# Layer 1's last sums: which queue loads the partial sums and stores the final rows

## The chip, the cores and the metric

The kernel runs on one core of one Trainium2 chip. The metric is device time of one execution in microseconds (us). The engines are called by their short names: PE is TensorE (PEld its weight loads), DVE is VectorE, ACT is ScalarE, POOL is GpSimd, SP is SyncE. SP computes nothing here: it waits for semaphores and issues transfers. A transfer can be issued by SP, by ACT or by POOL; each engine handles its own instructions strictly in order, so a wait in front of one instruction holds everything behind it.

## The reference

The input is 4 batches of 2048 tokens with 256 values each. Two half-weight mixture-of-experts layers stand around one attention layer:

```
x = x + 0.5 * ffn(layernorm(x))      # layer 0
x = x + attention(layernorm(x))
x = x + 0.5 * ffn(layernorm(x))      # layer 1, gives the result
# ffn: two of 16 experts for each token, mixed by softmax of the two router scores, plus a shared expert
# attention: the first 256 tokens attend causally to themselves, the other 1792 to 64 compressed tokens
```

So each row of the result is (row before layer 1) + 0.5 x (shared expert) + two expert results with their weights.

## The kernel before

A batch is handled as 8 *pairs* (`PB`), a pair being 2 x 128 rows of 256 values, 256 KB. The work runs in 16 phases in the order of a plan, with a fence between them. A phase T (tokens) normalises a batch's rows, routes them and computes the shared expert; it stores x + shared part in the DRAM tensor `partial_sums` (`acc_v`). A phase E (experts) takes the normalised rows by slot, in pairs of slot pages, through their experts, and stores `slot_results`. A phase A (attention) first adds the two expert results of layer 0 to each row of a batch and then runs attention on it. The phase C at the end does the last sums of batch 3.

The last sums of the other batches, layer 1's rows, are hidden in other phases. For pair n of such a batch they are: load the partial sums into `last_x[n % 2]` (a part of `normalised_rows`), gather four blocks of 128 expert results into `last_gath[n % 2]` (for even n a part of `normalised_rows`, for odd n `gathered_last_results`), four instructions of DVE (`last_sum`, at L1273 and L1278, which count `last_out`), and store the finished pair to `out`. Two places do them:

- the attention phase of batch 3, here called **A3**, does the 16 pairs of batches 0 and 1. DVE adds pairs 2i-2 and 2i-1 at the end of step i of its loop (i = 1 to 7) and pairs 14 and 15 after the loop. POOL also gathers layer 0's results for the attention's own rows there (`gathered_results`), two pairs ahead of their use;
- the second expert phase of layer 1, here called **E14**, does the 8 pairs of batch 2. DVE's loop body of four expert pairs ends with two sums in its last four turns. POOL gathers the rows of the expert pairs there too (L722), four ahead of PE, and puts a last pair behind every second one of them from pair 36 of 48 on.

In the kernel before, POOL does every transfer of the last sums. `last_pair(ph, n)` waits until pair n-2 is summed, stores it (L667), waits until that store has landed (`sums_stored`, since pair n is loaded over it), loads the partial sums of pair n (L680) and issues the four gathers of pair n (L655). SP has in A3 only the loads and stores of the attention's own rows, and in E14 nothing.

Of the kernel before, what the change touches and what calls it, by code (L numbers as in the profile page):

```python
# [35 lines left out]
PB = TB // 2  # L36
# [28 lines left out]
NS = 4  # L65
# [56 lines left out]
def macaron_kernel(nc, x_in, wq, wk, wv, wo, w1, b1, w2, b2, rw_t, rbias, up, gate, down,  # L122
                   shg_t, shu_t, shd_t, out, plan):
    ctx = ExitStack()
    with ctx:
# [254 lines left out]
        phases = []  # L380
# [81 lines left out]
        def _(sp):  # L462
# [19 lines left out]
            def store_rows(ph, i, s):  # L482
                sp.wait_ge(a_out.sem, a_out.done(ph["a"] + i))
                sp.dma_start(acc_v[ph["b"] * PB + i], outs[:, s]).then_inc(outs_stored[s].sem, 16)

            def load_tokens(ph, pairs):
# [43 lines left out]
            for ph in phases:  # L530
# [19 lines left out]
                if ph["kind"] == "T":  # L550
                    tokens(ph)
                elif ph["kind"] == "A":
                    for i in range(NS, PB):
                        load_rows(ph, i, i % NS)
                    for i in range(5, PB + 5):
                        if i == PB + 4:


                            sp.wait_ge(c_out.sem, c_out.done(ph["c"] + PB - 1))
                            for s in range(NS):  # L560
                                sp.wait_ge(outs_stored[s].sem, used(ph, s, s))
                            load_tokens(phases[ph["n"] + 1], range(NS))
# [13 lines left out]
        def _(gp):  # L576
# [82 lines left out]

            def last_pair(ph, n):  # L660

                lasts = ph["last"]
# [8 lines left out]
                if n < PB * len(lasts):  # L671
                    last, l = lasts[n // PB], lasts[0]["l"] + n
                    if n % PB == 0:
                        results_stored(1, last["b"])
                    if n == 0:
                        gp.wait_ge(phase_done["pe"].sem, ph["n"])
                        for s in range(NS):
                            gp.wait_ge(norm_stored[s].sem, 32 * ph["tokens_before"])
                    gp.wait_ge(sums_stored[n % 2].sem, 8 * (l - n % 2))
                    gp.dma_start(last_x[:, n % 2], acc_v[last["b"] * PB + n % PB]).then_inc(sums_in[n % 2].sem, 16)  # L680
                    gather_pair(last_gath[n % 2], last_in[n % 2], 1, last["b"], n % PB)

            def gather(ph):

# [6 lines left out]
                        for n in range(2 * i - 8, 2 * i - 6):  # L691
                            last_pair(ph, n)
                if ph["last"]:
                    for n in range(PB, PB * len(ph["last"]) + 2):
                        last_pair(ph, n)

            def gather_all(ph):
# [11 lines left out]
            def slot_rows(ph):  # L709
# [16 lines left out]
                            last_pair(ph, (i - begin) // 2)  # L726
                    first += part["pairs"]
                if ph["last"]:
                    for n in range((ph["pairs"] - begin) // 2, PB + 2):
                        last_pair(ph, n)  # L730

            def build(ph, n):
# [1181 lines left out]
```

## Time and profile before

| | |
|---|---|
| three runs, median (lowest to highest) | 2016.77 us (2015.26 to 2021.91) |
| the profiled execution, its own time | 2013.89 us |
| its span in the trace | 2012.2 us |
| PE busy | 1480.4 us (74%) |
| DVE busy | 1047.0 us (52%) |
| POOL busy | 876.3 us (44%) |
| chain that ended last | PE 53%; DVE 14%; POOL 13%; issue 10%; DMA 4% |
| stores to `out` by POOL (DMA out<-normalised_rows) in that chain | 3.0% |

Busy times overlap; no engine is busy through the whole span, so the time is made of stretches with different limits. The chain is the sequence of work in which each piece was released by the one before it; what stands in it sets the time. POOL's rows for a transfer give how long POOL took to issue it, not how long the data travelled.

### The profile page before, as it was taken

The page shows a single profiled execution, that of the slowest core. Times are in us where ns is not written, and L with a number is a line of the kernel's source. Part 1 is how long each engine was busy: PE and PEld are TensorE (multiplying, and loading weights), DVE is VectorE, ACT ScalarE, POOL GpSimd, SP SyncE. Part 2 cuts the span into 40 slices and gives each one's busy share as a digit, 9 for nine tenths or more (in the row PEclk, how much of TensorE's full clock was granted, in tenths as well). Part 3 has the DMA queues.
Part 4 walks back from the last instruction along what each step waited for, and adds up shares of the span by engine and source line. Part 5 has one row for each costly group of instructions (what it writes and reads, how often), then busy time and mean ns, then how long its engine had stood idle before and what let it go on. Part 6 is the DMA issues. An engine that isn't in the chain of part 4 may idle for free.

```text
span 2012.2 us, 35562 instructions
## 1 busy us (share of the span) xinstructions
PE 1480.4 (74%) x11274; PEld 1247.8 (62%) x11275; DVE 1047.0 (52%) x3253; ACT 617.5 (31%) x1254; POOL 876.3 (44%) x1108
## 2 busy tenths in 40 slices
PE   4797787999967779578767779698674447799650
PEld 3787677988854548455654559587543327698540
DVE  4657546544434755556734766243553547474332
ACT  2333223444423323233212323244321103244220
POOL 4563486655532200210272006655135463756656
PEclk9897798999976889688877889799786767799775
DMA  4732224556541122210231021356223352256555
GB/s 116 225 104 65 84 79 126 167 164 157 161 136 43 48 74 74 81 39 24 90 121 43 27 74 63 107 160 156 84 64 110 105 157 77 87 156 176 147 146 170
DMA packets 166002, 215.71 MB, mean 107 GB/s; under 512 B 18800, under 2 KB 143856, under 8 KB 165872
## 3 DMA queue, kind: packets, MB, share of 16 engines
q0 software_dynamic: 32256, 90.22, 17.0%
q1 hardware_dynamic: 87920, 79.74, 12.3%
q10 hardware_dynamic: 45696, 44.05, 6.6%
q8 instruction: 78, 1.28, 0.3%
q14 instruction: 52, 0.43, 0.1%
HBM read 119.56 MB, written 94.37 MB: 106 GB/s over the span
## 4 chain that ended last, share of the span: by engine, by line
PE 53%; DVE 14%; POOL 13%; issue 10%; DMA 4%; ACT 4%; another core or an unknown queue 2%; ACTq 0%; DVEq 0%; POOLq 0%; SPq 0%
PE bank L1444 8%; PE bank L1455 7%; PE bank L1594 7%; PE bank L1457 6%; PE bank L1456 6%; PE bank L1515 4%; DMA out<-normalised_rows 3%; POOL queries_high L739 2%; POOL normalised_rows L655 2%; POOL gathered_last_results L655 2%; DVE bn_stats L1042 2%; POOL rows_and_results L722 2%; PE bank L1846 2%; DVE score_maxima L1328 2%
## 5 line engine op out<-in xcount | busy, mean ns | idle before, releaser
L722 POOL DMA_INDIRECT rows_and_results<-normalised_by_token,rows_of_slots x336 | 319.7, 952 | 215.4 <-PE bank L1444 131.5
L655 POOL DMA_INDIRECT gathered_results<-slot_results,slot x128 | 122.0, 953 | 389.4 <-DVE combined_rows L1278 282.8
L1226 DVE TENSOR_TENSOR rows_transposed_low<-bank,rows_transposed_high 128x512 fp32r<-128x512 f32 x168 | 116.0, 691 | 270.2 <-ACT rows_transposed_high L812 178.6
L1455 PE MATMUL bank<-expert_gate_up_high,rows_transposed_high 128*128 x672 | 210.3, 313 | 47.1 <-DVE rows_transposed_low L1226 27.1
L737 POOL TENSOR_SCALAR keys_high<-iota,place_in_page_of_choice 128x128 fp32r<-128x128 f32 x96 | 57.6, 600 | 330.1 <-DVE place_in_page_of_choice L1165 322.7
L1456 PE MATMUL bank<-expert_gate_up_low,rows_transposed_high 128*128 x672 | 194.3, 289 | 0.0
L1457 PE MATMUL bank<-expert_gate_up_high,rows_transposed_low 128*128 x672 | 194.1, 289 | 0.0
L1594 PE MATMUL bank<-expert_down,hidden_work 128*128 x672 | 186.6, 403 | 0.5
L1455 PEld LDWEIGHTS bank<-expert_gate_up_high,rows_transposed_high 128*128 128x128 f32 x672 | 132.8, 198 | 60.0 <-issue 58.5
L1455 PE MATMUL bank<-rows_transposed_high,shared_gate_up_high 128*128 128x256 f32 x512 | 159.1, 311 | 0.3 <-DVE hidden_work L1001 0.3
L1444 PE MATMUL bank<-identity,hidden_work 128*128 128x128 f32 x464 | 96.8, 308 | 78.0 <-ACT hidden_work L766 29.8
L1456 PE MATMUL bank<-rows_transposed_low,shared_gate_up_high 128*128 128x256 f32 x512 | 152.8, 298 | 0.0
L1457 PE MATMUL bank<-rows_transposed_high,shared_gate_up_low 128*128 128x256 f32 x512 | 152.6, 298 | 0.0
L812 ACT ACTIVATE rows_transposed_high<-bank 128x512 fp32r<-128x512 f32 x168 | 100.4, 598 | 154.6 <-ACT rows_and_results L827 65.5
L827 ACT ACTIVATE rows_and_results<-bank 128x512 f32<-128x512 f32 x168 | 100.5, 598 | 153.8 <-PE bank L1594 129.8
L1456 PEld LDWEIGHTS bank<-expert_gate_up_low,rows_transposed_high 128*128 128x128 f32 x672 | 133.3, 198 | 0.0
L1594 PEld LDWEIGHTS bank<-expert_down,hidden_work 128*128 128x128 f32 x672 | 120.8, 200 | 19.1 <-issue 8.2
L1457 PEld LDWEIGHTS bank<-expert_gate_up_high,rows_transposed_low 128*128 128x128 f32 x672 | 132.7, 197 | 0.0
L1444 PE MATMUL bank<-identity,rows_and_results 128*128 128x128 f32 x672 | 109.0, 288 | 23.2 <-DMA rows_and_results<-normalised_by_token,rows_of_slots 23.2
L1515 PE MATMUL bank<-shared_down,hidden_work 128*128 128x256 f32 x512 | 121.3, 380 | 0.0
L766 ACT ACTIVATE normalised_rows<-rows_and_results,minus_mean_by_deviation,rstd 128x256 f32<-128x256 f32 x128 | 68.7, 591 | 155.5 <-DVE minus_mean_by_deviation L1081 146.7
L739 POOL TENSOR_SCALAR queries_high<-iota,page_of_choice,token_of_batch_plus_one 128x48 fp32r<-128x48 f32 (+2 forms) x192 | 115.9, 604 | 0.0
(277 smaller groups left out, 3754.9 us busy)
## 6 DMA issues: line engine op xcount, KB each, us to landing
slot_results<-rows_and_results ACTq DMA_DIRECT2D x168, 256.0 KB
partial_sums<-rows_and_results SPq DMA_DIRECT2D x96, 256.0 KB, 2.1
rows_and_results<-partial_sums SPq DMA_DIRECT2D x72, 256.0 KB, 4.3
normalised_by_token<-normalised_rows SPq DMA_DIRECT2D x64, 256.0 KB, 2.5
rows_and_results<-in_L_attn_hidden_states SPq DMA_DIRECT2D x32, 256.0 KB, 3.3
normalised_rows<-partial_sums POOLq DMA_DIRECT2D x24, 256.0 KB
out<-normalised_rows POOLq DMA_DIRECT2D x24, 256.0 KB, 2.7
rows_and_results<-normalised_by_token,rows_of_slots POOLq DMA_INDIRECT x336
```

The lines of the kernel that those rows point to most:

```text
L655: gp.indirect_dma_start(into[:, t, k, :], None, ys[part], bass.IndirectOffsetOnAxis(ap=slot[:, b, k, 2 * i + t:2 * i + t + 1], axis=0))\
L722: gp.indirect_dma_start(rows[:, i % NS, t, :], None, norm_d, bass.IndirectOffsetOnAxis(ap=listed[:, page:page + 1], axis=0))\
L739: gp.tensor_scalar(page_one[n % BUILT][:, 0:width], iota_f[:, 0:width], pagef[:, k, t:t + 1], token_f[:, t:t + 1], ALU.is_equal, ALU.mult) ...
L812: act.activation(flat(xt_h[:, k]), bank[k][:], ACT.Copy)\
L827: act.activation(flat(outs[:, s]), bank[6 + s % 2][:], ACT.Copy)\
L1226: dve.tensor_tensor(flat(xt_l[:, k]), bank[k][:], flat(xt_h[:, k]).bitcast(F32), ALU.subtract)\
L1444: return pe.transpose(out_, in_, ident[:])
L1455: pe.matmul(out_, lh, rh, start=first, stop=False)
L1456: pe.matmul(out_, lh, rl, start=False, stop=False)
L1457: return pe.matmul(out_, ll, rh, start=False, stop=last)
L1515: m = pe.matmul(bank[6 + s % 2][:, t * D:(t + 1) * D], work[:, 1 + i % 2, h, t * P:(t + 1) * P], sd[:, h, :], start=h == 0, stop=h == SH / ...
L1594: m = pe.matmul(bank[6 + k][:, t * D:(t + 1) * D], ht[:, k, t * P:(t + 1) * P], ed[:, ds(e, 1), :].rearrange("p a d -> p (a d)"), start=Tr ...
```

## The change

The loads of the partial sums and the stores of the finished rows go from POOL to SP. POOL keeps the gathers; in front of the gathers of pair n it now waits only until pair n-2 is summed. SP gets `load_sum` and `store_sum`. In A3 it puts two of each between two stores of the attention's rows; in E14 it runs them through in a loop of its own. The loads of pairs 0 and 1 are issued at once. What is computed, the buffers and DVE's order are as before.

```diff
+            def load_sum(ph, n):
+                last, l = ph["last"][n // PB], ph["last"][0]["l"] + n
+                if n == 0:
+                    for s in range(NS):
+                        sp.wait_ge(norm_stored[s].sem, 32 * ph["tokens_before"])
+                sp.wait_ge(sums_stored[n % 2].sem, 8 * (l - n % 2))
+                sp.dma_start(last_x[:, n % 2], acc_v[last["b"] * PB + n % PB]).then_inc(sums_in[n % 2].sem, 16)
+
+            def store_sum(ph, n):
+                last, l = ph["last"][n // PB], ph["last"][0]["l"] + n
+                sp.wait_ge(last_out.sem, last_out.done(l))
+                sp.dma_start(out_v[last["b"] * PB + n % PB], last_x[:, n % 2]).then_inc(sums_stored[n % 2].sem, 16)
...
                 elif ph["kind"] == "A":
...
-                    for i in range(5, PB + 5):
-                        if i == PB + 4:
...
-                        store_rows(ph, i - 5, (i - 5) % NS)
+                    if ph["last"]:
+                        load_sum(ph, 0)
+                        load_sum(ph, 1)
+                    for i in range(PB - 1):
+                        if i:
+                            store_rows(ph, i - 1, (i - 1) % NS)
+                        if ph["last"]:
+                            for n in (2 * i, 2 * i + 1):
+                                store_sum(ph, n)
+                                load_sum(ph, n + 2)
+                    store_rows(ph, PB - 2, (PB - 2) % NS)
+                    next_tokens(ph)
+                    store_rows(ph, PB - 1, (PB - 1) % NS)
+                    if ph["last"]:
+                        for n in (2 * PB - 2, 2 * PB - 1):
+                            store_sum(ph, n)
+                elif ph["kind"] == "E" and ph["last"]:
+                    load_sum(ph, 0)
+                    load_sum(ph, 1)
+                    for n in range(PB):
+                        store_sum(ph, n)
+                        if n + 2 < PB:
+                            load_sum(ph, n + 2)
...
             def last_pair(ph, n):
...
-                def store(n):
-                    last, l = lasts[n // PB], lasts[0]["l"] + n
-                    gp.wait_ge(last_out.sem, last_out.done(l))
-                    gp.dma_start(out_v[last["b"] * PB + n % PB], last_x[:, n % 2]).then_inc(sums_stored[n % 2].sem, 16)
...
                 if n >= 2:
-                    store(n - 2)
...
-                    gp.wait_ge(sums_stored[n % 2].sem, 8 * (l - n % 2))
-                    gp.dma_start(last_x[:, n % 2], acc_v[last["b"] * PB + n % PB]).then_inc(sums_in[n % 2].sem, 16)
-                    gather_pair(last_gath[n % 2], last_in[n % 2], 1, last["b"], n % PB)
+                    gp.wait_ge(last_out.sem, last_out.done(l - 2))
+                gather_pair(last_gath[n % 2], last_in[n % 2], 1, last["b"], n % PB)
```

`next_tokens` holds the waits and loads that stood under `if i == PB + 4`, unchanged.

POOL's instructions in A3 before the change, from the gathers of last pair 1 to the load for last pair 4 (L667 is the store, L680 the load of partial sums, `gathered_results` the attention's own gathers):

```order
L655 DMA gathered_last_results<-slot_results0,slot 128x256 x4
L655 DMA gathered_results<-slot_results1,slot 128x256 x4
L667 DMA out<-normalised_rows 128x2x256
L680 DMA normalised_rows<-partial_sums 128x2x256
L655 DMA normalised_rows<-slot_results0,slot 128x256 x4
L667 DMA out<-normalised_rows 128x2x256
L680 DMA normalised_rows<-partial_sums 128x2x256
L655 DMA gathered_last_results<-slot_results0,slot 128x256 x4
L655 DMA gathered_results<-slot_results1,slot 128x256 x4
L667 DMA out<-normalised_rows 128x2x256
L680 DMA normalised_rows<-partial_sums 128x2x256
```

The same place of POOL after the change, where all gathers are L689:

```order
L689 DMA gathered_last_results<-slot_results0,slot 128x256 x4
L689 DMA gathered_results<-slot_results1,slot 128x256 x4
L689 DMA normalised_rows<-slot_results0,slot 128x256 x4
L689 DMA gathered_last_results<-slot_results0,slot 128x256 x4
L689 DMA gathered_results<-slot_results1,slot 128x256 x4
```

The stores and loads are gone from between the gathers, and 12 gathers in a row stand where two stores and two loads parted them.

SP's instructions in A3 before the change, where L480 loads the attention's rows, L484 stores them and L489 loads the next phase's rows:

```order
L480 DMA rows_and_results<-partial_sums 128x2x256 x8
L484 DMA partial_sums<-rows_and_results 128x2x256 x7
L489 DMA rows_and_results<-partial_sums 128x2x256 x4
L484 DMA partial_sums<-rows_and_results 128x2x256
L489 DMA rows_and_results<-partial_sums 128x2x256 x4
```

SP's first instructions in A3 after the change, with L492 the load and L497 the store of a last sum:

```order
L480 DMA rows_and_results<-partial_sums 128x2x256 x8
L492 DMA normalised_rows<-partial_sums 128x2x256 x2
L497 DMA out<-normalised_rows 128x2x256
L492 DMA normalised_rows<-partial_sums 128x2x256
L497 DMA out<-normalised_rows 128x2x256
L492 DMA normalised_rows<-partial_sums 128x2x256
L484 DMA partial_sums<-rows_and_results 128x2x256
L497 DMA out<-normalised_rows 128x2x256
L492 DMA normalised_rows<-partial_sums 128x2x256
```

Each L484 from the first on now has two stores and two loads of last sums ahead of it, and the stores of pairs 14 and 15 stand between the last L484 and the last loads of the next phase's rows.

## Rows read from the trace of the kernel before

**Rows 1.** Chain of waits in A3: start us, us, what.

```profile
1508.37 2.92 DMA out<-normalised_rows
...
1530.41 2.69 DMA gathered_results<-slot_results,slot
...
1537.53 2.57 DMA out<-normalised_rows
...
1559.25 2.73 DMA gathered_results<-slot_results,slot
...
1569.35 2.58 DMA out<-normalised_rows
```

**Rows 2.** Who waited for whom, 1430 to 1665 us: total us, times, longest.

```profile
POOL normalised_rows L680 <- DMA out<-normalised_rows: 33.7, 14, 4.1
```

**Rows 3.** Busy us of PE, PEld, DVE, ACT, POOL; then clock, DMA share, GB/s.

```profile
1508.00:1662.00 154.00, 67.65 (x596) 45.76 (x596) 71.83 (x155) 22.09 (x45) 84.31 (x93) 0.69 0.40 124
1853.00:1958.00 105.00, 62.78 (x356) 54.36 (x355) 35.45 (x83) 24.18 (x48) 64.48 (x70) 0.77 0.55 152
```

**Rows 4.** Timeline of POOL in A3: start us, us, instruction, idle before it.

```profile
1556.74 0.95 POOL L655 DMA_INDIRECT gathered_results<-slot_results,slot  x1 [0.30 <-issue]
...
1587.20 0.76 POOL L667 DMA_DIRECT2D out<-normalised_rows  x1
...
1605.25 0.76 POOL L667 DMA_DIRECT2D out<-normalised_rows  x1
```

**Rows 5.** Timeline of DVE in two attention phases, batch 2's (1146 to 1195) and A3.

```profile
1146.64 2.48 DVE L1328 TENSOR_REDUCE score_maxima<-bank 128x8 f32<-128x512 f32 x4
...
1154.36 0.69 DVE L1313 TENSOR_TENSOR rows_transposed_low<-bank,rows_transposed_high 128x512 fp32r<-128x512 f32 x1 [1.56 <-ACT rows_transposed_high L864]
...
1176.67 2.48 DVE L1328 TENSOR_REDUCE score_maxima<-bank 128x8 f32<-128x512 f32 x4 [3.72 <-PE bank L1816]
...
1194.98 0.69 DVE L1355 TENSOR_TENSOR rows_and_results<-bank,combined_rows 128x512 f32<-128x512 f32 x1 [3.34 <-PE bank L1673]
...
1570.56 2.48 DVE L1328 TENSOR_REDUCE score_maxima<-bank 128x8 f32<-128x512 f32 x4
...
1581.44 0.69 DVE L1313 TENSOR_TENSOR rows_transposed_low<-bank,rows_transposed_high 128x512 fp32r<-128x512 f32 x1 [4.73 <-ACT rows_transposed_high L864]
```

**Rows 6.** Timeline of DVE at A3's end and the next phase's start.

```profile
1663.14 0.87 DVE L1278 SCALAR_TENSOR_TENSOR normalised_rows<-gathered_last_results,weights,normalised_rows 128x256 f32<-128x256 f32 x2
...
1668.41 0.16 DVE L1081 SCALAR_TENSOR_TENSOR minus_mean_by_deviation<-mean,rstd 128x4 f32<-128x4 f32 x1
```

**Rows 7.** Who waited for whom, 1800 to 2012 us (E14's end and C).

```profile
POOL normalised_rows L680 <- DMA out<-normalised_rows: 17.1, 6, 4.0
```

**Rows 8.** Timeline of POOL in E14, around the first last pair, and the last gather.

```profile
1850.61 0.95 POOL L722 DMA_INDIRECT rows_and_results<-normalised_by_token,rows_of_slots  x1 [0.94 <-PE bank L1444]
...
1949.98 0.95 POOL L655 DMA_INDIRECT gathered_last_results<-slot_results,slot  x1 [0.30 <-issue]
```

**Rows 9.** Timeline of DVE in E14, the sums of pairs 1, 5, 6 and 7.

```profile
1875.32 0.87 DVE L1278 SCALAR_TENSOR_TENSOR normalised_rows<-gathered_last_results,weights,normalised_rows 128x256 f32<-128x256 f32 x2
...
1932.51 0.88 DVE L1278 SCALAR_TENSOR_TENSOR normalised_rows<-gathered_last_results,weights,normalised_rows 128x256 f32<-128x256 f32 x2
...
1945.90 0.87 DVE L1273 SCALAR_TENSOR_TENSOR normalised_rows<-normalised_rows,weights 128x256 f32<-128x256 f32 x2
...
1954.00 0.88 DVE L1278 SCALAR_TENSOR_TENSOR normalised_rows<-gathered_last_results,weights,normalised_rows 128x256 f32<-128x256 f32 x2
```

**Rows 10.** Timeline of SP in A3: one store of attention rows.

```profile
1652.06 0.36 SPq L484 DMA_DIRECT2D partial_sums<-rows_and_results  x1
```

**Rows 11.** Us from issue to landing: SP's loads, POOL's stores, SP's four loads together.

```profile
rows_and_results<-partial_sums SPq DMA_DIRECT2D x72, 256.0 KB, 4.3
...
DMA to landing us min/median/max: 2.6/2.7/4.6
...
DMA to landing us min/median/max: 5.3/5.3/5.3
```

More of the change, by code:

```diff
@@ L484, in store_rows, with next_tokens @@
                 sp.dma_start(acc_v[ph["b"] * PB + i], outs[:, s]).then_inc(outs_stored[s].sem, 16)
+            def load_sum(ph, n):
[9 more added lines that the diff above has]
+                sp.dma_start(out_v[last["b"] * PB + n % PB], last_x[:, n % 2]).then_inc(sums_stored[n % 2].sem, 16)
+            def next_tokens(ph):
+                sp.wait_ge(c_out.sem, c_out.done(ph["c"] + PB - 1))
+                for s in range(NS):
+                    sp.wait_ge(outs_stored[s].sem, used(ph, s, s))
+                load_tokens(phases[ph["n"] + 1], range(NS))
             def load_tokens(ph, pairs):
@@ L554, in _ @@
                         load_rows(ph, i, i % NS)
-                    for i in range(5, PB + 5):
-                        if i == PB + 4:
[L559 to L562, printed above, removed]
-                        store_rows(ph, i - 5, (i - 5) % NS)
+                    if ph["last"]:
[21 more added lines that the diff above has]
+                            load_sum(ph, n + 2)
                 elif ph["kind"] == "C":
@@ L660, in last_pair @@
             def last_pair(ph, n):
-                lasts = ph["last"]
-                def store(n):
-                    last, l = lasts[n // PB], lasts[0]["l"] + n
-                    gp.wait_ge(last_out.sem, last_out.done(l))
-                    gp.dma_start(out_v[last["b"] * PB + n % PB], last_x[:, n % 2]).then_inc(sums_stored[n % 2].sem, 16)
-                if n >= 2:
-                    store(n - 2)
[L671 to L678, printed above, removed]
-                    gp.wait_ge(sums_stored[n % 2].sem, 8 * (l - n % 2))
-                    gp.dma_start(last_x[:, n % 2], acc_v[last["b"] * PB + n % PB]).then_inc(sums_in[n % 2].sem, 16)
-                    gather_pair(last_gath[n % 2], last_in[n % 2], 1, last["b"], n % PB)
+                last, l = ph["last"][n // PB], ph["last"][0]["l"] + n
+                if n % PB == 0:
+                    results_stored(1, last["b"])
+                if n == 0:
+                    gp.wait_ge(phase_done["pe"].sem, ph["n"])
+                    for s in range(NS):
+                        gp.wait_ge(norm_stored[s].sem, 32 * ph["tokens_before"])
+                if n >= 2:
+                    gp.wait_ge(last_out.sem, last_out.done(l - 2))
+                gather_pair(last_gath[n % 2], last_in[n % 2], 1, last["b"], n % PB)
             def gather(ph):
@@ L693, in gather @@
                 if ph["last"]:
-                    for n in range(PB, PB * len(ph["last"]) + 2):
+                    for n in range(PB, PB * len(ph["last"])):
                         last_pair(ph, n)
@@ L728, in slot_rows @@
                 if ph["last"]:
-                    for n in range((ph["pairs"] - begin) // 2, PB + 2):
+                    for n in range((ph["pairs"] - begin) // 2, PB):
                         last_pair(ph, n)
```

## The prediction

> **What bounds the kernel now.** I read the whole chain of waits first. It is mixed, but it has two long stretches in which PE hardly occurs and POOL's gathers alternate with stores to `out`: A3 from 1508 us to its end at 1664, and E14 from 1853 to 1955. The busy time by stretch [rows 3] shows why they are worth a look: POOL is the busiest engine in both (84.3 of 154 us, 64.5 of 105), PE is idle for much of them, and its granted clock is a mean of 0.69 and 0.77, between its two levels of 1.2 and 2.4 GHz. No engine is full, so a loop of waits sets the pace.
>
> The chain of A3 [rows 1] shows the loop. DVE finishes pair 0 and POOL stores it at 1508.37. The twelfth gather behind that store, the last one for the attention's own pair 6, is issued at 1530.41. DVE takes it 2.7 us later, adds pair 6, then the last sums 2 and 3, and the next store goes out at 1537.53. The waits [rows 2] price POOL's part: 14 times it stood until a store had landed before it could load over it, 33.7 us. In E14 POOL waits the same way 6 times, 17.1 us [rows 7].
>
> **What POOL loses, per last pair.** One gather takes 0.95 + 0.30 = 1.25 us of POOL [rows 4], four are 5.0 us. A store and a load cost the rest: two stores of neighbouring pairs stand 18.05 us apart for two pairs [rows 4], 9.0 per pair, so 4.0 us per pair go to store, landing and load. Those 4 us leave POOL for all pairs that have a store ahead of them.
>
> **A3, cycle by cycle.** Nothing changes before 1508.37, since pair 0's sum is released by attention work. Then:
>
> - *Step 1 to 2.* Twelve gathers in a row: the last is issued 11 x 1.25 = 13.8 us behind the release, 14.0 with a slower first one, where it now takes 1530.41 - 1508.37 = 22.0. That saves 8.0. *Step 2 to 3*: 1559.25 - 1537.53 = 21.7 against 14.0, 7.7 more. What is late next, DVE's own step, is 11.6 us from its maxima to its split of the transposed rows (1570.56 to 1581.44 + 0.69 [rows 5]) and about 1.2 before that, 12.8, still under 14.0 + 2.7. So the gathers still set the pace, and the store at 1569.35 [rows 1] becomes a release at about 1553.6.
> - *Step 4.* POOL now has only last pairs, 8 gathers or 10 us a step. Pair 7's last gather is issued at 1553.6 + 8.8 and lands by 1565.1. DVE starts its maxima at 1570.56 - 15.7 = 1554.9; from there to the end of the split is 8.4 us in the attention phase of batch 2, which has no last sums (1146.64 to 1154.36 + 0.69), and 11.6 in A3, where PE had cooled down [rows 5]. A last sum is two instruction pairs of 0.8 us, 1.6. I take the nearer condition, a PE that waits less: 1554.9 + 8.4 + 3.2 = 1566.5. DVE has become the bound.
> - *Step 5* the same, 11.6 more, 1578.1. *Step 6* has no split; pair 11's gathers end 0.3 + 8.8 + 2.7 = 11.8 us behind the release by sum 8 (1576.5), so 1588.3, and sum 11 is done at 1589.9. *Step 7 and the end*: from step 7's maxima to the last attention sum batch 2 needs 1194.98 + 0.69 - 1176.67 = 19.0 us [rows 5]; sums 12 and 13 fit into DVE's idle time in it (pair 13 has landed by about 1598), 14 and 15 come behind: 1589.9 + 19.0 + 3.2 = 1612.1.
>
> The phase now ends at 1663.14 + 0.87 = 1664.0 [rows 6]. That saves 51.9 us. With 11.6 instead of 8.4 in two steps it is 45.5; with landings of 4.6 instead of 2.7 us [rows 11] in the four places where gathers still bind, another 7.6 goes. I take 50.
>
> **E14.** Until the first last pair POOL keeps up: an expert pair takes it two gathers and a wait for PE, 0.94 + 0.95 + 0.30 + 0.95 = 3.14 us [rows 8]. From 1850.61 + 2.5 = 1853.1 on, 54 gathers are left (32 of last pairs, 22 of expert pairs). In a row the last would be issued at 1853.1 + 53 x 1.25 = 1919.4, against 1949.98. That 30.6 us is the most there is. Two other limits take some back. The sum of pair 1 (done at 1876.2 [rows 9]) was not late by its gathers, so POOL may slip some 2.5 us against expert pairs that aren't transposed yet. And after the sum of pair 5 DVE has four expert pairs to do before pair 6's: 1945.90 - 1933.4 = 12.5 us [rows 9]. Pair 5's last gather is the 44th: 1853.1 + 53.8 + 2.7 = 1909.6, sum done at 1911.2 to 1913.7; then 12.5 and 3.2: sum 7 is done at 1926.9 to 1929.4, against 1954.00 + 0.88 = 1954.9. That saves 25.5 to 28, I take 27. PE's floor (12 pairs x 3.14 + 8 sums x 1.6 = 50.6 us) is far below these 75. What follows, results stored and then C, has its own gathers and keeps its length.
>
> **What is added to SP.** It gets 24 loads and 24 stores, each some 0.4 us of its queue (0.36 in [rows 10]), which is nearly idle here. The cost lies in the order. In A3 each store of attention rows (L484) now stands behind two waits for landed stores. DVE waits for such a store only four pairs later, so it has a step's worth of cover and more. At the end, the store of pair 6's rows waits for the store of sum 13 to land: about 1599.7 + 0.4 + 2.7 + 0.4 = 1603.2, against some 1602 when the row is ready; the loads of the next phase's first rows go out behind it and land by 1611, 5.3 us at the slowest [rows 11]. They are needed at 1612. I cost it at 0; without that cover it is 1 to 3 us. The last store lands about 2.7 us after the phase, and ACT, which waits for it, needs the norms only 4.4 us after it (1664.0 to 1668.4 [rows 6]): 0.
>
> The load of pair n still waits until pair n-2 has been stored over the same buffer, now on SP. With a landing time of X, two pairs in a row are 3X + 3.8 us (a store, a load, a store, a load, three landings in series, 2.2 us of issue and release, the sum's 1.6). At 2.7 us, POOL's median for such stores [rows 11], this is 11.9, beside gathers that need 11.8 + 1.6: hidden, and I cost it at 0. SP's own loads take 4.3, but most are issued in bunches.
>
> **The rule that speaks against it.** The rows say that a store lands 2.7 us after POOL's issue, and as late as 4.6 behind gathers in E14 and A3 [rows 11], which could come from standing in POOL's queue. The Trainium skill (DMA: Bandwidth & Descriptors, "Queues, rings and completion order") says that a transfer's semaphore increment lands only after every earlier write of the same DMA engine, across its queues. By that, a store on SP would be held up by gathers as much as one on POOL. The trace cannot tell, as no store to `out` has left SP beside gathers. What it would do here is the second rival.
>
> **Sum.** 50 + 27 = 77 us from the profiled execution's 2013.9 gives 1936.9. The median of the runs is 2.9 us above that execution; I forecast between the two bases, 1938.
>
> **Rivals.**
>
> - *DVE's steps stay slow in A3*, because PE still waits for the sums and its clock stays low. Steps 4 to 6 then take 11.6 + 3.2 = 14.8: step 7 starts at 1554.9 + 44.4 = 1599.3, the end is at 1621.5, saving 42.5; with 25.5 in E14 that is 68: 1946. For it: 11.6 is what A3 shows. Against: PE's idle time in A3 shrinks from 86 us to under 40.
> - *Landings on SP are as long as its longest row, 5.3 us.* A step is 19.7 us. A3 from 1508.4: two steps of about 23, five of 19.7, 144.5 where it is 155.6 now; E14 from sum 1 to sum 7: 3 x 19.7 = 59.1 against 78.7. It saves 31: 1983. For it: the DMA engines' busy share [rows 3] rises, 0.40 x 154 us over 104 us is 0.59, 0.55 x 105 over 78 is 0.74. Against: stores in the chain of A3 are 2.6 to 2.9 beside the same gathers.
> - *Slower.* The same chain turns into a loss where ten steps take more than the present 155.6 + 78.7 = 234.3 us: 23.4 each, X = 6.5. At 7.0 it would be 2013.9 + 14 = 2028. No row shows such landings.
> - *No change*, the store waits having been hidden anyway: [rows 1] puts them on the chain, hence next to nothing.
>
> **How the numbers follow.** The forecast's case (1930 to 1943) 0.62; slow steps and somewhat longer landings (1943 to 1957) 0.23; the SP chain (1957 to 1995) 0.07; below 1930, if E14 gives the full 30.6 and PE is warm throughout, 0.05; no change 0.01; slower 0.02. The range for 8 in 10 is 1929 to 1957. A measurement of this kernel can tell about 0.3% (6 us) from no change: faster 0.97, same 0.01, slower 0.02.
>
> **What would show it.** Right: in A3 the distance between neighbouring releases of POOL falls from 29 and 32 us to about 21 and 24, then about 12; A3 ends near 1612 and E14's sum 7 comes some 77 us before 1954.9; no POOL instruction waits for a store; PE's clock in both stretches is higher. Wrong: DVE's sums wait for the loads of partial sums instead of the gathers (SP chain), landings of stores to `out` above 4 us, DVE idle in A3's steps 4 to 6 while it waits for ACT (slow steps), or the next phase's first norms waiting for rows that SP loaded late.

## The result and the profile after

The changed kernel took 1985.61 us (median of 4 runs, 1981.44 to 1993.37) against 2016.01 us (4 runs, 2014.29 to 2021.91): a ratio of 0.9856, 95% interval 0.9835 to 0.9877. It is faster by 1.4%, or 29 us by that ratio (the medians are 30.4 us apart), where the forecast had 77. Predicted were 1938 us and a range of 1929 to 1957; the result lies outside. The profiled execution took 1987.23 us, its span is 1985.5 us, 26.7 less than before.

In the kernel after, POOL's gathers of the attention's own rows and of the last pairs are L689, those of expert pairs L746, SP's load of partial sums L492 and its stores L497 (to `out`) and L484; ACT's exponentials are L907, its copies of queries and maxima L893 and L898; DVE's last sums L1297 and L1302.

What the change was to remove is gone: no instruction of POOL waits for a store. The busy times by stretch, columns as in [rows 3], show POOL down from 84.3 us in 154 to 61.1 in 138, and a clock that has hardly risen in A3 (0.69 before):

```profile
1509.00:1647.00 138.00, 65.98 (x596) 43.70 (x596) 73.06 (x160) 22.20 (x45) 61.06 (x64) 0.72 0.46 139
1838.00:1943.00 105.00, 66.93 (x361) 55.05 (x359) 35.58 (x82) 25.24 (x50) 56.04 (x59) 0.83 0.55 161
```

The page's fourth part, the shares of the chain that ended last, has something that the rows before the prediction didn't show, 6% for "another core or an unknown queue" on a kernel that has one core (2% before):

```profile
PE 54%; DVE 16%; issue 11%; POOL 6%; another core or an unknown queue 6%; ACT 5%; DMA 1%; ACTq 0%; DVEq 0%; POOLq 0%; SPq 0%
```

In the chain of A3 (start us, us, what), which answers to [rows 1], these pieces are where the stores to `out` stood; with one of 0.74 us they are 61.7 us of 138:

```profile
1514.62 11.77 another core or an unknown queue
...
1538.78 12.10 another core or an unknown queue
...
1566.48 6.20 another core or an unknown queue
...
1582.72 7.07 another core or an unknown queue
...
1592.34 8.21 another core or an unknown queue
...
1602.01 15.62 another core or an unknown queue
```

Who waited is in the timeline of ACT in A3 (start us, us, instruction, idle before it and its releaser); "remote" means that the semaphore which it waited for was incremented just then, but that no instruction or transfer ends near that time:

```profile
1514.59 0.38 ACT L898 ACTIVATE score_maxima_transposed<-bank 128x256 fp32r<-128x256 f32 x1 [5.35 <-issue]
1526.37 2.06 ACT L907 ACTIVATE raw_weights<-bank 128x512 f32<-128x512 f32 x4 [11.39 <-remote]
...
1550.87 2.06 ACT L907 ACTIVATE raw_weights<-bank 128x512 f32<-128x512 f32 x4 [11.73 <-remote]
...
1617.62 2.07 ACT L907 ACTIVATE raw_weights<-bank 128x512 f32<-128x512 f32 x4 [15.24 <-remote]
```

PE had finished the scores for the first of them at 1516.57:

```profile
1516.15 0.42 PE L1754 MATMUL bank<-score_maxima_transposed,minus_by_head 32*128 32x256 f32 x4
...
1527.12 2.01 PE L1870 MATMUL bank<-raw_weights,compressed_values 128*32 128x256 f32 x7 [9.51 <-ACT raw_weights L907]
```

The trace's own records of semaphores say what ACT waited for. These four matmuls of PE make four increments; they end at 1516.57 at the latest, by the trace's model of their ends, and the increments are recorded at 1526.35, 1526.38, 1526.42 and 1526.45. ACT starts within 0.1 us of the first. So ACT isn't late by itself: PE's word comes 9.8 us late. An instruction of DVE that ended at 1516.83, in the same burst, has its increment at 1516.84. Before the other four long waits of ACT's exponentials in A3 PE's first increment is recorded 10.2, 4.2, 5.8 and 14.3 us behind the modelled end. In all fifteen traces every wait above 1.5 us that is laid on nobody, of whatever engine, is one for an increment of PE. In this text a *stall* is such a wait.

POOL's timeline shows what surrounds it: first and last gather of the burst, one every 1.25 us with nothing between, and the release of the next one:

```profile
1509.45 0.94 POOL L689 DMA_INDIRECT normalised_rows<-slot_results,slot  x1 [29.69 <-DVE normalised_rows L1302]
...
1523.21 0.94 POOL L689 DMA_INDIRECT gathered_results<-slot_results,slot  x1 [0.30 <-issue]
1533.86 0.95 POOL L689 DMA_INDIRECT normalised_rows<-slot_results,slot  x1 [9.71 <-DVE normalised_rows L1302]
```

ACT goes on 2.2 us behind the end of that burst (1524.15 to 1526.37). The other long waits before the exponentials also end 1.5 to 2.8 us behind the end of one, and the longest, 15.24 us, stands beside the longest burst, 16 gathers from 1594.91 to 1614.83. One wait of 8.3 us, before the copy of the queries at 1600.63, ended inside that burst, so not every one lasts until the burst is over. Before the change a store and its landing parted the gathers after every four or eight.

A3 ends at 1646.7 instead of 1664.0 [rows 6]. In E14, POOL's first and last gather of a last pair:

```profile
1838.87 0.95 POOL L689 DMA_INDIRECT normalised_rows<-slot_results,slot  x1 [0.30 <-issue]
...
1915.23 0.95 POOL L689 DMA_INDIRECT gathered_last_results<-slot_results,slot  x1 [0.30 <-issue]
```

### The profile page after: what moved, and what is told of

It reads as the page before. It is cut to its first block, busy times and chain, and to the rows that moved or that the text cites. A ratio compares the mean times of both kernels' runs of the same rounds, so it can differ in the third digit from the quotient of the medians.

```text
span 1985.5 us, 35564 instructions
## 1 busy us (share of the span) xinstructions
PE 1483.1 (75%) x11274; PEld 1248.2 (63%) x11275; DVE 1046.6 (53%) x3253; ACT 617.9 (31%) x1254; POOL 836.3 (42%) x1060
## 4 chain that ended last, share of the span: by engine, by line
PE 54%; DVE 16%; issue 11%; POOL 6%; another core or an unknown queue 6%; ACT 5%; DMA 1%; ACTq 0%; DVEq 0%; POOLq 0%; SPq 0%
PE bank L1468 8%; PE bank L1479 7%; PE bank L1618 7%; PE bank L1480 6%; PE bank L1481 6%; PE bank L1539 4%; POOL queries_high L763 2%; DVE bn_stats L1066 2%; DVE score_maxima L1352 2%; PE bank L1870 2%; PE bank L1813 2%; ACT raw_weights L907 1%; PE bank L1697 1%; DVE score_maxima L1409 1%
## 5 line engine op out<-in xcount | busy, mean ns | idle before, releaser
L746 POOL DMA_INDIRECT rows_and_results<-normalised_by_token,rows_of_slots x336 | 319.3, 950 | 223.2 <-PE bank L1468 134.7
L689 POOL DMA_INDIRECT gathered_results<-slot_results,slot x128 | 121.7, 951 | 389.8 <-DVE combined_rows L1302 282.0
L851 ACT ACTIVATE rows_and_results<-bank 128x512 f32<-128x512 f32 x168 | 100.5, 598 | 145.9 <-PE bank L1618 124.7
L1870 PE MATMUL bank<-raw_weights,compressed_values 128*32 128x256 f32 x448 | 88.3, 466 | 52.4 <-ACT raw_weights L907 52.1
L1468 PE MATMUL bank<-identity,rows_and_results 128*128 128x128 f32 x672 | 109.7, 289 | 23.6 <-DMA rows_and_results<-normalised_by_token,rows_of_slots 22.8
```

The source lines that it names most:

```text
L689: gp.indirect_dma_start(into[:, t, k, :], None, ys[part], bass.IndirectOffsetOnAxis(ap=slot[:, b, k, 2 * i + t:2 * i + t + 1], axis=0))\
L746: gp.indirect_dma_start(rows[:, i % NS, t, :], None, norm_d, bass.IndirectOffsetOnAxis(ap=listed[:, page:page + 1], axis=0))\
L851: act.activation(flat(outs[:, s]), bank[6 + s % 2][:], ACT.Copy)\
L1468: return pe.transpose(out_, in_, ident[:])
L1870: pe.matmul(bank[6][group[g], cols], flat(vc[:, 4 * c + g]), pt[:, g, cols], start=True, stop=True)
```

## The experiments

Two theories were put to the test. *Bursts*: while POOL issues gathers back to back, ACT's next start is held up until the burst ends (by the records above, through PE's late increments). *Transfers*: it is SP's new loads and stores, or the traffic on the DMA engines. A first pair of runs tells how the gain divides.

A length of A3 is from the start of DVE's first last sum there to the start of its last instruction pair of sums; one of E14 is from POOL's first gather of a last pair to its first gather of C. "Stalls" are ACT's remote waits between those two points of A3, in full, so with the time that ACT would have waited for PE anyway. A, E and C are the kinds of phases; "all places" are the gathers of last pairs in A3 and E14 and the own gathers of the four attention phases. Times differ from chip to chip (the kernel before took 2015.3 to 2026.9 us), so each ratio is to the kernel before on the same chip.

| kernel | us | ratio (95%) | A3 | stalls | E14 |
|---|---|---|---|---|---|
| before (profiled) | 2016.01 | 1 | 156.7 | 8.0 | 109.7 |
| changed | 1985.61 | 0.9856 (0.9835-0.9877) | 138.4 | 59.9 | 99.8 |
| A3 only | 2004.54 | 0.9943 (0.9918-0.9968) | 140.6 | 52.4 | 111.8 |
| E14 only | 2006.46 | 0.9957 (0.9939-0.9975) | 156.8 | 8.0 | 100.9 |
| changed, waits for landings in A3 | 1974.48 | 0.9803 (0.9772-0.9835) | 133.8 | 0 | 98.0 |
| changed, no last gathers in A3 | 1944.41 | 0.9641 (0.9617-0.9666) | 89.2 | 0 | 101.4 |
| changed, narrow gathers | 1999.37 | 0.9868 (0.9845-0.9891) | 137.5 | 47.5 | 99.1 |
| changed, 10 memsets in A3 | 1978.95 | 0.9766 (0.9740-0.9791) | 126.5 | 0 | 100.3 |
| changed, 4 memsets in A3 | 1973.76 | 0.9739 (0.9717-0.9762) | 119.3 | 15.3 | 100.3 |
| waits for landings, all attention phases | 1951.87 | 0.9624 (0.9599-0.9649) | 134.6 | 0 | 100.5 |
| changed, 4 memsets in E14 | 1981.85 | 0.9817 (0.9792-0.9842) | 138.2 | 59.1 | 95.1 |
| 4 memsets, all places | 1931.15 | 0.9574 (0.9538-0.9610) | 121.0 | 10.9 | 95.2 |
| 1 memset, all places | 1975.71 | 0.9783 (0.9760-0.9807) | 130.8 | 37.2 | 100.9 |
| 3 memsets every 2 gathers, all places | 1920.66 | 0.9512 (0.9482-0.9543) | 124.5 | 0 | 94.0 |
| before, 3 memsets every 2 gathers | 1992.06 | 0.9881 (0.9857-0.9906) | 175.0 | 0 | 119.8 |

### One part of the change alone

In the first kernel POOL's `last_pair` is that of before unless the phase is an A, in the second unless it is an E; SP's part follows, and the two places get semaphores of their own.

```diff
+                if ph["kind"] != "A":        # "E" in the second kernel
+                    return last_pair_all(ph, n)   # as in the kernel before
```

> SP does the loads and stores in A3 only; in E14 POOL does them as in the kernel before. The prediction's sum (50 us saved in A3) would give 1966 us. The burst theory (ACT's work stands still while POOL issues gathers back to back, 50.9 us of such stalls in A3 after the change against 8.0 before) says the gain of A3 is only what its own end shows, DVE 1664.0 to 1646.7, so 16 to 18 us: 1999 us, with ACT's long stalls before the exponentials in A3 again and none new in E14.

> SP does the loads and stores in E14 only; A3 as in the kernel before. The prediction's term (27 us saved in E14) would give 1989 us. The traces say C began 25.0 us earlier after the change where E14's last pairs began 13.9 us earlier, so 11 us net: 2005 us. If 1989 comes out, E14 is worth its full term and A3 gave next to nothing.

Measured: 2004.54 us, a ratio of 0.9943 or 11 us on this chip, and 2006.46 us, 0.9957 or 9 us. By the traces the first saves 16.1 us of A3 and loses 2.1 in E14, the second saves 8.8 in E14. Both terms are far below their forecasts of 50 and 27, and both at about what the changed kernel's trace says (18.3 and 9.9). The first is 5.5 us above what the burst theory expected (1999), the second 1.5 us (2005). Added up the two gains are 20 us of the changed kernel's 29; the intervals leave room for most of that difference. A3's stalls are there again, 52.4 us of them.

### A pause for landings, and the gathers left out

```diff
                 gather_pair(last_gath[n % 2], last_in[n % 2], 1, last["b"], n % PB)
+                if ph["kind"] == "A":
+                    gp.wait_ge(last_in[n % 2].sem, (l - n % 2) * 32 + 64)
```

> The changed kernel, and in A3 POOL waits after the four gathers of every last pair until these have landed, so no more than eight gathers follow each other. Burst theory: ACT's stalls before the exponentials end in the first such pause (some 7 us into a burst and not after its end), their sum in A3 falls from 50.9 us to under 30 us, and A3 gets no longer although POOL waits some 3 us per last pair: 1975 to 1985 us. Theory of the transfers (SP's loads and stores, not the gathers, hold ACT up): the stalls stay at 45 to 55 us, POOL's waits come on top: 1990 to 2005 us.

Measured: 1974.48 us, and no remote wait at all in A3. POOL waits longer and the kernel gets faster, though A3 itself only by 4.6 us (138.4 to 133.8), as POOL's waits take most of it back. Its timeline and ACT's:

```profile
1504.45 0.95 POOL L689 DMA_INDIRECT normalised_rows<-slot_results,slot  x1 [0.30 <-issue]
1508.17 0.94 POOL L689 DMA_INDIRECT gathered_last_results<-slot_results,slot  x1 [2.77 <-DMA normalised_rows<-slot_results,slot]
```

```profile
1505.85 0.38 ACT L900 ACTIVATE score_maxima_transposed<-bank 128x256 fp32r<-128x256 f32 x1 [5.35 <-PE bank L1470]
1507.85 2.06 ACT L909 ACTIVATE raw_weights<-bank 128x512 f32<-128x512 f32 x4 [1.62 <-PE bank L1756]
```

Between the copy of the maxima and the exponentials lie 2.0 us, where the changed kernel has 11.8 (1514.59 to 1526.37).

The second kernel leaves the gathers out:

```diff
+                if ph["kind"] == "A" and n >= 2:
+                    return
...
-                dve.wait_ge(last_in[s].sem, (l - s) * 32 + 64)
+                if ph["kind"] == "E":
+                    dve.wait_ge(last_in[s].sem, (n - s) * 32 + 128)
+                elif n < 2:
+                    dve.wait_ge(last_in[s].sem, 64)
```

> The changed kernel without the gathers of last pairs 2 to 15 in A3 (56 gathers left out, DVE adds what lies in the buffers, so these rows of the result are not the reference's); SP's loads and stores are all there. Burst theory: no ACT stall over 6 us after the phase's first gathers, and A3 runs at DVE's steps of 11.6 us or a little more: 35 to 45 us less than the changed kernel, 1941 to 1951 us. Theory of the transfers: SP's loads and stores hold ACT up as before, the stalls stay at 40 us or more and the time at 1975 us or more.

Measured: 1944.41 us, no stalls in A3, 49.2 us less of it (138.4 to 89.2). All of SP's loads and stores are in this kernel, so by themselves they hold nothing up. The theory of the transfers has lost SP's half.

### Less data, and breaks without idleness

For the narrow gathers the same number of instructions moves a quarter of the bytes:

```diff
-                            into[:, t, k, :], None, ys[part],
+                            into[:, t, k, 0:wide], None, ys[part].rearrange("r (q d) -> (r q) d", d=wide),
...
+                            D // 4 if ph["kind"] == "A" and n >= 2 else D)
```

> The changed kernel with the gathers of last pairs 2 to 15 in A3 a quarter as wide (rows of 64 values, so these rows of the result are not the reference's); as many gathers, at the same pitch on POOL. If it is the issuing of gathers back to back that holds ACT up, the stalls stay (45 to 55 us in A3, 1980 to 1990 us). If it is the data that they move (the DMA engines' traffic), the stalls shrink with it to under 20 us and the time goes to 1945 to 1960 us.

Measured: 1999.37 us, 0.9868, the changed kernel's ratio, with 47.5 us of stalls. One of them:

```profile
1533.79 2.06 ACT L908 ACTIVATE raw_weights<-bank 128x512 f32<-128x512 f32 x4 [11.41 <-remote]
```

It is not the bytes that the gathers move. As many gathers of as many rows are still issued, so a limit by the number of rows isn't excluded. Next, POOL stays busy but issues no gather for a moment:

```diff
                 gather_pair(last_gath[n % 2], last_in[n % 2], 1, last["b"], n % PB)
+                if ph["kind"] in "A":
+                    for _ in range(10):           # 4 in the second kernel
+                        made(gp.memset(filler[:], 0.0))
```

> The changed kernel, and in A3 POOL does ten small memsets, one after the other, behind the four gathers of every last pair: POOL is never idle but issues no gather for some 2 us. Issue theory: ACT's stalls end in these gaps as they did with the wait for the landings, their sum is under 30 us and the time 1970 to 1980 us. If POOL has to be idle, or the gathers have to have landed, for ACT to go on, the stalls stay at 45 us or more and the time is 1985 to 2000 us.

> As the one before with four memsets, a gap of some 0.8 us. If any break in the gathers lets ACT through, this is the faster one: 1960 to 1975 us with stalls under 20 us. If the break has to last until what was issued has been worked off (ACT's stalls ended 1.5 to 2.8 us behind the last gather), it is too short: stalls of 40 us or more, 1980 to 1990 us.

Measured: 1978.95 us (0.9766) without stalls, and 1973.76 us (0.9739) with 15.3 us of them. The short break, POOL's timeline:

```profile
1516.59 0.94 POOL L690 DMA_INDIRECT normalised_rows<-slot_results,slot  x1 [0.30 <-issue]
1517.52 0.64 POOL L709 MEMSET filler<- 128x16 f32 x4
1518.77 0.95 POOL L690 DMA_INDIRECT gathered_last_results<-slot_results,slot  x1 [0.61 <-issue]
```

The next gather starts 2.2 us after the last instead of 1.25; these 0.9 us cut most of the stalls. POOL need not be idle, and the last gather need not have landed: the memsets are over 1.6 us after that gather's start, where the wait for landings took 3.7 from start to start. So it is the unbroken issuing of gathers, not POOL's being busy. The longer break has no stalls and is still no faster; by the traces its A3 is 7.2 us longer.

### Breaks in the other places

Every attention phase of the kernel before had such a stall as well, beside its first 12 gathers. Its ACT and POOL in batch 0's phase:

```profile
643.42 1.26 ACT L925 ACTIVATE raw_weights<-bank 128x384 f32<-128x384 f32 x3 [13.82 <-remote]
```

```profile
626.23 0.95 POOL L655 DMA_INDIRECT gathered_results<-slot_results,slot  x1 [25.94 <-DVE combined_rows L1278]
...
640.29 0.95 POOL L655 DMA_INDIRECT gathered_results<-slot_results,slot  x1 [0.30 <-issue]
```

```diff
                     gather_pair(gath[:, c % 2], gathered[c % 2], 0, ph["b"], i)
+                    gp.wait_ge(gathered[c % 2].sem, (c - c % 2) * 32 + 64)
```

> The kernel with the wait for landings behind every last pair of A3 (1974.5 us), and the same wait behind each four gathers of the attention's own rows, in all four attention phases, which each show one ACT stall of 12 to 16 us beside their first 12 to 16 gathers. Burst theory: these four stalls fall to 7 us or less, 6 to 9 us saved in each phase if the stall is on the path there: 1940 to 1960 us. If the stall in the self-attention is something else, they stay and the time is 1970 to 1980 us.

This edit comes on top of the waits in A3's last pairs. Measured: 1951.87 us, 0.9624, that is 0.018 or 36 us below the kernel with these waits in A3's last pairs alone. A3's first last sum begins at 1477.69 there, against 1507.51 in the changed kernel. The next kernel has the four memsets in E14 alone (`ph["kind"] in "E"`):

> The changed kernel with four small memsets behind every last pair's gathers in E14 alone; A3 as changed. If E14 gave back part of its forecast 27 us by the same thing (ACT stalls of 3 to 7 us in POOL's stream of 54 gathers, and the last expert pairs late after them), ACT's stalls there shrink and the ratio to the kernel before falls from 0.9856 to 0.976 to 0.981 (10 to 20 us less than the changed kernel). If E14 ends by POOL's stream or by the experts' own length, nothing is gained: ratio 0.984 to 0.988.

Measured: 1981.85 us, 0.9817, 8 us below the changed kernel, with overlapping intervals; E14 is 4.7 us shorter. That lies between the two expectations, so breaks of this kind recover only a part of E14's shortfall.

> Four small memsets behind every four gathers of the attention phases (last pairs and own rows, all four phases) and behind every last pair in E14. A3's part alone gave a ratio of 0.9739; the attention's own gathers with waits for landings brought another 0.018 (0.9803 to 0.9624 on other chips). If the breaks act in each place apart: ratio 0.950 to 0.960. If one of the places has another limit: 0.960 to 0.970.

> As the one before with a single memset (some 0.2 us) in each place. If what lets ACT through is that POOL starts an instruction that is no gather, one will do: ratio equal to or up to 0.003 below the one with four. If it is the length of the break (0.9 us was enough, none is not), one is too short and the stalls come back: ratio 0.975 to 0.99.

Their edits are the memsets shown, with `in "AE"` and after the own gathers too. Measured: 1931.15 us, 0.9574 with four, within the expectation for places that act apart; 1975.71 us, 0.9783 with one. One memset makes the distance between two gathers 1.35 us, and the stalls are back, 37.2 us in A3. It still gives 15 us against the changed kernel, where four give 57, so it does a part of it: POOL's starting something else is not enough, and how long the break has to be lies between 0.1 and 0.9 us. (The profiled execution took 1986.16 us, the slowest of five, so its trace may show more stalls than is usual.)

```diff
                             .then_inc(sig.sem, 16)
+                    for _ in range(3):       # in gather_pair, behind every two gathers
+                        made(gp.memset(filler[:], 0.0))
```

> Three small memsets behind every two gathers instead of four behind every four, in the same places. If with four gathers in a row a part of the stall is still there (ACT's copy of the maxima and its exponentials now start 1 to 2.5 us late), shorter bursts take it away and the ratio is 0.002 to 0.006 below the one with breaks every four gathers. If the stall only begins after five or more gathers, it costs POOL time alone: the same or up to 0.005 above.

Measured: 1920.66 us, 0.9512 (0.9482 to 0.9543), the fastest of all: 98 us below the kernel before on its chip. ACT has no stall in A3, although POOL issues its gathers more slowly. By the traces the gain over four memsets isn't in A3, which is 3.5 us longer (121.0 to 124.5): A3's first last sum begins 11.7 us earlier (1473.94 to 1462.20), and E14 is 1.2 us shorter. In other places ACT still has stalls above 1.5 us, 61.7 us in the whole kernel against 188.9 in the changed one and 138.4 in the kernel before.

### The kernel before with the same breaks

The same edit in the kernel before asks what the change is worth when ACT isn't held up.

> The kernel before the change with three small memsets behind every two gathers of gather_pair, as in the changed kernel that reached 0.9512. It asks what the change is worth when the gathers no longer hold ACT up. If the forecast's sum for A3 and E14 was right but for the stalls, this kernel is 60 us or more slower than that one: a ratio to the kernel before of 0.981 or above. If the breaks give as much to the kernel before as to the changed one (98 us against 68 from the changed kernel's 0.9856), the change itself is worth some 30 us in either company: ratio 0.963 to 0.970.

Measured: 1992.06 us, 0.9881, so the first of the two expectations. The difference of the two ratios is 0.0369, 74 us. By the traces the change takes 175.0 - 124.5 = 50.5 us from A3 and 119.8 - 94.0 = 25.8 from E14, against forecasts of 50 and 27. That is nearer than it deserves: in this kernel POOL is more of a bound than in the kernel before, as its breaks come on top of the stores (A3 18.3 us longer than before, E14 10.1). What made it faster all the same is that A3's first last sum begins 50 us earlier (1456.53 against 1506.40), by the attention phases. The waits that the change removes are still all there (total us, times, longest), as in [rows 2]:

```profile
POOL normalised_rows L683 <- DMA out<-normalised_rows: 32.9, 14, 3.2
```

## Why the prediction was wrong

**What bounds the kernel.** Right. Both stretches were set by a loop in which POOL's stores stood, and both got shorter when these were taken out.

**What POOL loses per last pair.** Right: twelve gathers took 13.8 us from the first to the last (1509.45 to 1523.21), as worked out, and POOL waits for no store.

**A3, steps 1 to 3.** Here the sum failed first. "The last is issued 11 x 1.25 = 13.8 us behind the release", and that happened; but the step took 24.4 us (1509.45 to 1533.86) instead of 21.2, and the next 27.5 instead of 24.1. The limit named as late next, "DVE's own step", was counted without PE and ACT being touched by what POOL does. In place of the landing of the last gather, PE's late increments and, behind them, ACT's late exponentials now set the step.

**A3, steps 4 to the end.** This is the step that cost the most. From the release by sum 4 to the end the forecast had 1612.1 - 1553.6 = 58.5 us; it took 1646.7 - 1561.3 = 85.4, of the 34.6 us missing at A3's end 26.9. The forecast took the 8.4 us of batch 2's phase and put A3's 11.6 down to PE that had cooled down. Most of the 3.2 us between them had another cause in plain sight. ACT in that very step of the kernel before, and POOL beside it:

```profile
1578.85 2.06 ACT L883 ACTIVATE raw_weights<-bank 128x512 f32<-128x512 f32 x4 [3.99 <-remote]
```

```profile
1573.26 1.02 POOL L655 DMA_INDIRECT normalised_rows<-slot_results,slot  x1 [0.30 <-issue]
...
1577.13 0.95 POOL L655 DMA_INDIRECT normalised_rows<-slot_results,slot  x1 [0.30 <-issue]
1578.08 0.76 POOL L667 DMA_DIRECT2D out<-normalised_rows  x1
```

Four gathers, and ACT went on 0.8 us behind the last of them; PE's increment for it is recorded 2.4 us behind the modelled end. With eight to sixteen in a row the same stall grew to between 5.8 and 15.2 us. The kernels with the gathers left out, narrowed and broken up show it: without gathers A3 takes 89.2 us, less than the 1612.1 - 1506.4 = 105.7 forecast; with breaks of 0.9 us it takes 119.3. No run reached the forecast's length with all gathers in: 13.6 us stay, beside breaks that cost POOL 0.9 us per last pair and 15.3 us of stalls. The releases of POOL, which were to be 21, 24 and then about 12 us apart, came 24.4, 27.5, 17.0 and 16.6 us apart.

**E14.** The term was 27, measured are 9.9 by the stretch and 9 by the kernel with E14 alone. "In a row the last would be issued" 53 x 1.25 = 66.3 us after the first; it took 76.4 (1838.87 to 1915.23). The 10 us are in POOL's own waits before expert pairs (waits from 1838 to 1940 us):

```profile
ACT hidden_work L843 <- remote: 14.4, 3, 7.2
...
POOL rows_and_results L746 <- remote: 9.8, 5, 2.2
```

These are the same thing again, with POOL as the one who waits. PE's matmul (the last of four) and POOL behind its six gathers:

```profile
1841.37 0.60 PE L1468 MATMUL bank<-identity,rows_and_results 128*128 128x128 f32 x4
```

```profile
1848.23 0.95 POOL L746 DMA_INDIRECT rows_and_results<-normalised_by_token,rows_of_slots  x1 [2.15 <-remote]
```

The increment that POOL needs is recorded at 1847.97, 6.0 us behind the matmul's modelled end; before its other four waits of this kind it is 4.0 to 4.4 us. The forecast took POOL's wait for PE from a place without last pairs (3.14 us per expert pair) and let it vanish in the row of 54. Its floor for PE was worked out with the same 3.14 us, which is POOL's pace and no time of PE's, so it showed nothing about PE.

And the last sum was done 16 us behind the last gather instead of 7.5 to 10, as DVE stood 7.05 us before its last four expert pairs, behind ACT. The breaks in E14 gave back 4.7 us, more frequent ones 5.8 (99.8 to 94.0). The rest of the 17 us missing there was not recovered by any run; that the breaks take POOL time as well may be a part of it, which isn't shown.

**SP's additions.** Costed at 0, and no cost is seen: DVE waited not once for a load in A3. The landings weren't all as short as assumed, though. The profile lays only four of SP's waits on stores (waits of SP from 1500 to 1650 us):

```profile
SPq L492 <- DMA out<-normalised_rows: 8.9, 4, 3.5
```

By SP's timeline each of the 14 loads that follow a store stood until that store had landed, 36.7 us in all, where POOL's waits were 33.7. They cost nothing that the traces show.

**The rule weighed.** From the issue of a store to `out` to the issue of the load that waits for it is 2.2 us for the first store in six of seven steps (1509.21 to 1511.37), and 3.4 to 4.5 us for the second in these, which has a load of SP's own just ahead of it (1511.78 to 1516.27); in the seventh step they are 3.1 and 2.7. POOL's stores had a median of 2.7. Five of the 14 are above 4 us, which the prediction names as a sign of being wrong; the sums didn't wait for them. By the Trainium skill (DMA: Bandwidth & Descriptors, "Queues, rings and completion order") an increment lands behind all earlier writes of its DMA engine. Six of the first stores leave room for such a hold-up of at most 2.2 us; what makes the second ones longer, gathers or the load ahead, no run here separates.

**The rivals.** The one with long landings on SP named 1983 us, next to the result, which would have been luck: it needs sums that wait for loads, and none did. The slow steps of DVE did happen (DVE waited for ACT 39.9 us in 5 waits in A3), but were priced at the 11.6 us of a step beside four gathers, and put down to PE's clock. The granted clock did stay low, 0.72 in A3 where it had been 0.69, so it may have a share; no run separates it. No rival said that POOL's gathers, once nothing parts them, would hold another engine up, and the range ended below such a case.

**What stays open.** What holds PE's increments back. The runs show when: beside unbroken gathers, whatever these move, and hardly or not at all beside the same number with breaks of 0.9 us or more. The records of semaphores exclude two explanations for the stalls of ACT: that ACT's next instruction came late (it started within 0.1 us of the increment, and POOL waited for PE in the same way), and that increments of all engines are late (DVE's came at once). Nor was program code being loaded in the first stall: from 1515 to 1526 us these were the only queues with transfers, none of them an instruction queue (queue: packets, MB, share of the DMA engines' time):

```profile
q0 software_dynamic: 472, 1.28, 38.6%
q1 hardware_dynamic: 604, 0.57, 17.3%
```

Whether PE's matmuls themselves end late or only their increments travel late, the trace can't say, as it models their ends. For the first speaks PE beside 12 gathers in batch 2's phase of the changed kernel, where it issued matmuls two at a time with a wait for nothing between them:

```profile
1082.74 0.38 PE L1815 MATMUL bank<-raw_weights,values 128*32 128x128 f32 x2 [0.83 <-issue]
1084.17 0.38 PE L1815 MATMUL bank<-hidden_work,values 128*32 128x128 f32 x2 [1.05 <-issue]
1085.61 0.58 PE L1815 MATMUL bank<-combined_rows_sixth,values 128*32 128x128 f32 x2 [1.06 <-issue]
```

That is argued from one place, not tried.

## What to carry to other kernels

Before costing a wait out of an engine's queue, ask what the wait did for the others: here the landings that parted POOL's gathers were also what let PE's results reach ACT. Look for waits that the trace lays on nobody, and see whether they share their start or end with something on another engine, and whose increment they were for; a stall of 4 us beside 4 gathers is a price for 12. When a queue is freed, the first run to make is one in which the freed engine does less or pauses: if the kernel gets faster by waiting, the bound has moved to an interference and not to an engine.

## What the runs showed of the hardware that was not expected

- Beside gathers that POOL issues back to back, one every 1.25 us, PE's semaphore increments were recorded 2.4 us (four gathers) to 14.3 us (sixteen) behind the modelled end of its matmuls. ACT's waits for them lasted up to 15.2 us in A3 and, before the exponentials, ended 1.5 to 2.8 us behind the last gather. POOL itself waited for such increments in E14.
- A quarter of the bytes per gather, in the last pairs of A3, changes nothing (47.5 us of stalls in A3, ratio 0.9868 against 0.9856).
- A break of 0.9 us after every four gathers removes most of the stalls (59.9 to 15.3 us), one of 0.1 us a smaller part (37.2 us left); it may be filled with memsets on POOL. Breaks every two gathers in the attention phases and in the last pairs of E14 made the changed kernel 3.5% faster (0.9856 to 0.9512).
- In A3, stores of 256 KB from SP landed within 2.2 us (six of 14), and within 3.4 to 4.5 us where a load of SP's stood just ahead (six).
